# A two-layer block for 32 short sequences on one core: one identity product per step, epsilon added on GpSimd, and a new order of all engines' work

## The reference

```python
# layer 1: a transformer block with modulation by c
shift1, scale1, gate1, shift2, scale2, gate2 = split(silu(c) @ w_ada + b_ada, 6)
k, q, v = split((ln(x) * (1 + scale1) + shift1) @ w_qkv, 3)      # 16 heads of 8 features
y = softmax(q / 8 @ k.T) @ v
x = x + gate1 * (y @ w_proj + b_proj)
x = x + gate2 * (gelu((ln(x) * (1 + scale2) + shift2) @ w_mlp1 + b_mlp1) @ w_mlp2 + b_mlp2)
# layer 2: graph attention, in two directions d, over the first 20 nodes
self = [x, c where the row sum of x is not 0] @ W_self.T + b_self
for d in 0, 1:
    A = adj if d == 0 else adj transposed over its two node axes
    w = softmax(where(A.sum(-1) > 0, q_d k_d / sqrt(8), -9e15) + A @ w_bias + b_bias)
    out_d = per head: (w @ self[:20]) @ Wout[d] + bout[d]
x = x + relu(self + out_0 + out_1)
# ln(x) = (x - mean) * rsqrt(var + 1e-6), over the 128 features
```

## Time and profile before

| | |
|---|---|
| three timed runs | 95.29, 95.89, 96.32 us (median 95.89) |
| the profiled execution, whole | 96.85 us |
| its span on the core | 95.1 us |
| PE busy | 82.7 us |
| DVE busy | 71.7 us |
| POOL busy | 49.0 us |
| ACT busy | 41.8 us |

### The profile page before, as it was taken

The page is one execution under the profiler, slowest core; times in us unless marked ns, Lnnn a source line. Parts: engine busy times, 40 slices in busy tenths (PEclk is TensorE's granted clock), DMA queues, the critical chain, the costliest instruction groups (busy, mean ns, idle before and its releaser), DMA issues.

```text
span 95.1 us, 4068 instructions
## 1 busy us (share of the span) xinstructions
PE 82.7 (87%) x1773; PEld 65.6 (69%) x1773; DVE 71.7 (75%) x181; ACT 41.8 (44%) x96; POOL 49.0 (52%) x60
## 2 busy tenths in 40 slices
...
DMA packets 3890, 5.75 MB, mean 60 GB/s; under 512 B 704, under 2 KB 3008, under 8 KB 3744
## 3 DMA queue, kind: packets, MB, share of 16 engines
...
...
HBM read 4.22 MB, written 0.52 MB: 50 GB/s over the span
## 4 chain that ended last, share of the span: by engine, by line
PE 74%; DVE 7%; issue 7%; ACT 4%; DMA 3%; POOL 1%; POOLq 1%; SPq 0%; ACTq 0%
PE ps_s L1030 12%; PE ps_b L971 7%; PE ps_b L945 7%; PE ps_b L965 7%; PE ps_b L894 5%; PE ps_b L1041 5%; PE ps_b L1066 5%; PE ps_b L1044 4%; PE ps_b L982 4%; PE ps_b L978 4%; DMA w_ada_sb<-in_w_ada 3%; PE ps_b L984 3%; PE ps_b L1074 2%; PE ps_b L921 2%; PE ps_b L953 2%
## 5 line engine op out<-in xcount | busy, mean ns | idle before, releaser
L1173 ACT ACTIVATE PT<-ps_b 120x384 f32<-120x384 f32 x16 | 7.2, 489 | 15.0 <-PE ps_b L1041 15.0
L755 POOL TENSOR_TENSOR Kb<-k_raw,head_mask 128x640 f32<-128x640 f32 x6 | 7.7, 1293 | 9.1 <-DVE k_raw L1273 4.7
L855 POOL TENSOR_TENSOR rstd<-var_eps,minus_half 128x2 f32<-128x2 f32 (+1 forms) x9 | 6.0, 671 | 8.6 <-DVE var_eps L1206 8.5
L723 POOL TENSOR_TENSOR E<-E,neg_max 128x640 f32<-128x640 f32 x7 | 8.9, 1271 | 0.9 <-DVE neg_max L1363 0.8
L1116 ACT ACTIVATE hidden<-ps_b,cols 128x256 f32<-128x256 f32 x16 | 7.1, 476 | 4.7 <-PE ps_b L965 4.7
L945 PE MATMUL ps_b<-xm,w_qkv_sb 128*128 128x256 f32 (+1 forms) x30 | 8.6, 418 | 0.0
L965 PE MATMUL ps_b<-xm,w_rest_sb 128*128 128x256 f32 x32 | 8.4, 381 | 0.0
L1066 PE MATMUL ps_b<-Vz,PT 120*32 120x54 f32 (+1 forms) x384 | 6.6, 216 | 2.1 <-issue 2.1
L1066 PEld LDWEIGHTS ps_b<-Vz,PT 120*32 120x32 f32 (+1 forms) x384 | 5.5, 116 | 4.0 <-issue 3.4
L1101 ACT ACTIVATE Kb<-ps_b,head_mask 128x256 f32<-128x256 f32 (+1 forms) x20 | 7.3, 440 | 1.9 <-PE ps_b L945 1.8
L1030 PE MATMUL ps_s<-Kb,home_b 32*32 32x80 f32 x512 | 8.0, 251 | 0.0
(11 more groups left out here) (109 smaller groups left out, 190.9 us busy)
## 6 DMA issues: line engine op xcount, KB each, us to landing
...
```

The source lines that it names most:

```text
L723: return engine.tensor_tensor(e, e, less_max(key), ALU.add)
L755: return engine.tensor_tensor(Kb1[:, m % K1_RING, d, :, 0:(g1 - g0) * UB, :].rearrange("p i b k -> p i (b k)"), k1_raw[:, d, bs, :].rearra ...
L1173: ins = act.activation(PT[0:KR, r, 0:CH, :], ps[0:KR, 0:CH * P].rearrange("p (j t) -> p j t", t=P), ACT.Exp)
```

## The change

- `rstd` on POOL now has two instructions: the epsilon is added there (then a wait for its own result, then the power), and DVE no longer has its epsilon instruction nor the wait before it.
- A `warm` step is one identity product, not two; there are 14 steps in place of 3, and `WARM` is 13 in place of 11.
- `ON`, `BANKS` and `ORDER` have new contents: every engine's work is ordered anew, and some stages have moved between DVE, ACT and POOL (below, those that the prediction speaks of).

```diff
-WARM = 11
-ON = {'adjf': 'pool',
+WARM = 13
+ON = {'adjf': 'act',
...
- 'resid1': 'pool',
+ 'resid1': 'dve',
...
- ('apply', 0): 'dve',
- ('bhead', 0): 'act',
- ('k1mask', (0, 1)): 'dve',
- ('k1mask', (1, 1)): 'dve',
...
+ ('adjf', 1): 'pool',
+ ('apply', 0): 'pool',
+ ('k1mask', (0, 0)): 'dve',
+ ('k1mask', (1, 0)): 'dve',
...
- ('spread', ('v1', 1, 0)): 'act',
- ('spread', ('v1', 2, 1)): 'act',
- ('spread', ('v1', 3, 1)): 'act',
+ ('shift', (0, 3)): 'dve',
+ ('spread', ('v1', 2, 0)): 'act',
...
- ('sub', 7): 'dve',
...
- ('zero', 'pad'): 'dve',
+ ('zero', 'v0_ones'): 'dve',
...
+ ('take', (('cmod', 0), 0)), ('rstd', (0, 2)), ('warm', 0), ('warm', 1), ('dense', ('xnT', 0)),
...
@@ -852,6 +852,7 @@
                     g0, g1 = norm_chunk(layer, p)
                     for s in fresh("pool", ("stats", key), ("consts", 0)):
                         pool.wait_ge(*s)
+                    wait_own(pool.tensor_scalar(var_eps[:, layer, g0:g1], meanvar[:, layer, g0:g1, 1], LN_EPS, None, ALU.add))
                     ins = pool.tensor_tensor(rstd[:, layer, g0:g1], var_eps[:, layer, g0:g1], minus_half[:, 0:g1 - g0],
                                              ALU.pow)
@@ -997,8 +998,7 @@
                 elif stage == "warm":
-                    for i in range(2):
-                        ins = pe.transpose(ps_s[:, i, 0:P], ident[:, :], ident[:, :])
+                    ins = pe.transpose(ps_s[:, key % HJ, 0:P], ident[:, :], ident[:, :])
@@ -1201,10 +1201,7 @@
                     ins = dve.bn_aggr(meanvar[:, layer, g, :], stats[:, layer, g, :])
-                wait_own(ins)
-                v = meanvar[:, layer, g0:g1, 1]
-                return dve.scalar_tensor_tensor(out=var_eps[:, layer, g0:g1], in0=v, scalar=LN_EPS, in1=v, op0=ALU.add,
-                                                op1=ALU.max)
+                return ins
```

More of the change, by code:

```diff
@@ L230 @@
  ('take', (('yT', 3), 0)): 'act',
[L231 to L234, removed]
- ('zero', 'pad'): 'dve',
+ ('ya', 0): 'dve',
+ ('ya', 4): 'dve',
+ ('ya', 6): 'dve',
+ ('zero', 'v0_ones'): 'dve',
  ('zero', 'v1_ones'): 'dve'}
 BANKS = {('cmod', 0): 0,
[L238 to L242, removed]
+ ('cmod', 1): 1,
+ 'qz': 2,
+ ('bias', 0): 3,
+ ('xnT', 0): 1,
+ ('q', 0): 3,
  ('k', 0): 2,
@@ L265 @@
  ('turn', 2): 1,
[L266 to L279, removed]
+ ('values', 2): 3,
+ ('turn', 3): 3,
+ ('turn', 4): 0,
+ ('values', 3): 0,
+ ('turn', 5): 3,
+ ('turn', 6): 0,
+ ('values', 4): 1,
+ ('turn', 7): 1,
+ ('turn', 8): 1,
+ ('values', 5): 2,
+ ('turn', 9): 2,
+ ('turn', 10): 0,
+ ('values', 6): 1,
+ ('turn', 11): 0,
  ('turn', 12): 0,
- ('values', 7): 0,
+ ('values', 7): 1,
  ('turn', 13): 1,
[L283 to L286, removed]
+ ('turn', 14): 3,
+ ('values', 8): 2,
+ ('turn', 15): 2,
+ ('turn', 16): 2,
  ('values', 9): 3,
@@ L290 @@
  ('values', 10): 1,
[L291 to L294, removed]
+ ('turn', 19): 2,
+ ('turn', 20): 2,
+ ('values', 11): 3,
+ ('turn', 21): 3,
  ('turn', 22): 0,
- ('values', 12): 3,
+ ('values', 12): 1,
  ('turn', 23): 1,
- ('yT', 0): 0,
- ('proj', 0): 0,
- ('x1tok', 0): 0,
+ ('yT', 0): 1,
+ ('proj', 0): 1,
+ ('x1tok', 0): 2,
  ('xn2T', 0): 0,
  ('mlp1', 0, 0): 2,
- ('mlp1', 0, 1): 1,
- ('mlp1', 0, 2): 0,
- ('mlp1', 0, 3): 0,
+ ('mlp1', 0, 1): 0,
+ ('mlp1', 0, 2): 1,
@@ L306 @@
+ ('mlp1', 0, 3): 1,
  ('mlp2', 0): 1,
[L307 to L310, removed]
+ ('rowsum', 0): 0,
+ ('self', 0): 2,
+ ('q1', 0, 0): 2,
+ ('k1', 0, 0): 3,
  ('q1', 0, 1): 1,
- ('k1', 0, 1): 2,
- ('v1', 0): 3,
- ('yT', 1): 1,
- ('proj', 1): 1,
- ('x1tok', 1): 3,
- ('xn2T', 1): 3,
- ('mlp1', 1, 0): 2,
- ('mlp1', 1, 1): 1,
- ('mlp1', 1, 2): 1,
- ('mlp1', 1, 3): 3,
- ('mlp2', 1): 2,
- ('rowsum', 1): 1,
- ('self', 1): 0,
- ('q1', 1, 0): 0,
- ('k1', 1, 0): 2,
- ('q1', 1, 1): 1,
@@ L328 @@
- ('k1', 1, 1): 0,
- ('v1', 1): 0,
- ('yT', 2): 3,
- ('proj', 2): 1,
- ('x1tok', 2): 2,
- ('xn2T', 2): 2,
- ('mlp1', 2, 0): 2,
- ('mlp1', 2, 1): 1,
- ('mlp1', 2, 2): 3,
- ('mlp1', 2, 3): 2,
+ ('k1', 0, 1): 0,
+ ('v1', 0): 1,
+ ('yT', 1): 3,
+ ('proj', 1): 3,
+ ('x1tok', 1): 2,
+ ('xn2T', 1): 2,
+ ('mlp1', 1, 0): 3,
+ ('mlp1', 1, 1): 0,
+ ('mlp1', 1, 2): 2,
+ ('mlp1', 1, 3): 1,
+ ('mlp2', 1): 0,
+ ('rowsum', 1): 0,
+ ('self', 1): 1,
+ ('q1', 1, 0): 1,
+ ('k1', 1, 0): 2,
+ ('q1', 1, 1): 0,
+ ('k1', 1, 1): 3,
@@ L338 @@
+ ('v1', 1): 3,
+ ('yT', 2): 0,
+ ('proj', 2): 3,
+ ('x1tok', 2): 3,
+ ('xn2T', 2): 3,
+ ('mlp1', 2, 0): 3,
+ ('mlp1', 2, 1): 0,
+ ('mlp1', 2, 2): 2,
+ ('mlp1', 2, 3): 1,
  ('mlp2', 2): 2,
  ('rowsum', 2): 3,
[L340 to L341 removed]
+ ('self', 2): 0,
+ ('q1', 2, 0): 0,
  ('k1', 2, 0): 0,
  ('q1', 2, 1): 3,
[L344 to L351 removed]
+ ('k1', 2, 1): 1,
+ ('v1', 2): 3,
```

236 lines of the change are left out of this document (118 added, 118 removed), and 12 rows, old and new, of the table ORDER.

## The result

The change makes the kernel slower. Its median is 99.31 us (98.88 to 102.59, 4 runs) beside 96.10 us for the kernel before: a ratio of 1.033, 95% interval 1.022 to 1.043. A second set of runs gave 1.026 (1.017 to 1.036). My forecast was 94.0 us, in a range of 92.6 to 96.6: wrong in size and in sign.

A forecast was written before the change was run, and what follows sets the result against it. PE was taken as the bound, with late waits for its own instruction blocks and a lowered clock. Terms -0.2 - 0.5 - 0.3 + 0.75 - 1.4 - 0.3 = -1.95 us gave 94.9 for the profiled execution, 94.0 median, range 92.6 to 96.6.

The forecast's parts named there:

- (a): Epsilon on GpSimd: each norm's latency moves by 0.0 to +0.3 us, counted inside (b), (d) and (e).
- (b): Front, 4.5 to 10 us: -0.2 us, with `apply` of chunk 2 later but fewer identity products ahead of k.
- (c): Layer-1 attention, to 26 us: -0.5 us, as the wait for the k evictions goes.
- (d): First norm of layer 2 (mid 1): -0.3 us if `nmr` gets in before `vmask`.
- rival 2: At mid 1, `vmask` on POOL holds `nmr` again, making (d) +1.3 us and the time 95.5; chance 0.27.
- (e): Norm of mid 2: +0.75 us, a PE wait that the change makes.
- (f): Last third: -1.4 us, with waits and clock costing 2.0 us instead of 3.4.
- The part on blocks of instructions: Last third: with a block every 3.7 us at best, only the third of five is short, by 0.8 us.
- the wait behind ACT's DMAs: Last third: ACT issues four DMAs between `exp` of units 8 and 23, so `values` 23 waits about 0.9 us.
- I leave the clock up: Last third: no clock loss counted, since waits are apart and shorter; a fall would cost 1.0 us again.
- (g): Tail: -0.3 us, with the last `ya` on DVE and transpose 3 under the `values`.
- Rival 1: Identity products raise the clock early, PE doing 10 to 13.5 us at 2.4 GHz: -0.7 us, 93.3; chance 0.10.

The follow-up runs named there:

- a_spread_sp: The changed kernel with the first half spread of mid 2 issued by SP and no longer by ACT; 99.40 us, ratio 1.014 to the kernel before.
- fixed: The changed kernel with `stats` 3 behind `nmr` 1, `nmr` of mid 2 behind mid 3's, `vmask` 4 earlier, half spread on SP; 95.72 us, ratio 0.978.
- fixed_few_id: The kernel of fixed with 11 identity products at the start and none later; 95.19 us, ratio 0.978 to the kernel before.
- a_stats: The changed kernel with `stats` of chunk 3 moved behind `nmr` of chunks 2 and 1 on DVE; 98.02 us.

## Why the prediction was wrong, point by point

(a) Epsilon. The instruction takes 0.23 us (I took 0.25). Calling it nothing by itself was wrong: 1.3% either way, depending on the order.

(b) Front, -0.2. The first scores came at 13.54 us, 13.64 before: right in sum, by the wrong sum, and so by luck. `stats` ahead of `nmr` costs 0.5 us and not 0.8 when the load is early (power ready at 6.44 us, `nmr` at 6.97) and over 3 us when it is late, which I left out: I read 4.5 us once as if it were fixed. The early clock gave 0.3 to 0.4 back.

(c) Layer-1 attention, -0.5. The 0.5 us wait went and 1.24 us of the same kind (k evictions) came ahead of the first scores. To the transposes of mid 1 (33.18, before 33.06) the changed kernel is level, although it waits 1.75 us there against 0.92. So about 0.7 us were gained by then, as (b) and (c) say together.

(d) **Mid 1, -0.3: failed, and it was rival 2.** I saw that power and `max` would end together and bet on `nmr`. `vmask` went first by 0.07 us, and it did so in all six profiles of kernels with this order: `nmr` took 2.05 or 2.06 us each time, and PE waited 1.75 us in five and 1.21 in one. That is no coin. What fits is that POOL needs no semaphore to go on and DVE waits for one, the argument that I had written down for the rival and then priced at 0.27. The Trainium skill (SBUF — State Buffer, SBUF: two separate sides) says that the port pair of GpSimd and VectorE is an exclusive lock for the whole instruction, taken by whichever starts first, where the VectorE operation has two inputs in SBUF and the GpSimd one reads SBUF, as here; the 2.05 us agree.

(e) Norm of mid 2, +0.75: too high. It is 0.24 us before mid 2 and 0.40 before mid 3, +0.4 in sum against the 0.22 of before. I had mid 3 done long before; it came directly ahead, and its wait took the other's.

(f) Last third, -1.4: **failed.** The part on blocks of instructions held: I gave 0.8 us for what is left of 2.11, and at that edge it is 0.55 to 1.10 in thirteen of the fourteen profiles of the changed family (in six of them 0.34 to 0.38 more one block on). Two parts failed.

The first is the wait behind ACT's DMAs. It was priced at 0.9 us from 3.28 us for four; they took 4.15 (one of them 1.62), and the wait was 2.03 to 2.09.

The second is "I leave the clock up", an expensive line. In the six profiles that have this wait, the clock falls within 1.5 us behind it in five. In the eight of the changed family without it, it does not fall between 19 and 89 us. But seven of those eight have it low in the tail, from some point between 89.8 and 93.5 us to the end, and in a_spread_sp, fixed and fixed_few_id that begins 1.7 to 2.3 us behind waits of 2.52, 1.90 and 1.54 us. Behind the 1.75 us of mid 1 it fell in two profiles of five, and in none where the wait is gone. In the family of the kernel before it fell within 1.0 us behind a block wait of 1.26 to 1.75 us in three profiles of four. Not each long wait is followed by a fall, so this is a chance and not a rule; but a wait of 2 us must be priced at 2 us plus that chance. I had argued the reverse from the kernel before, where two block waits went before one.

(g) Tail, -0.3: right (from the end of the last `values` to the end of the span 5.0 us against 5.3).

The sum against the earlier trace rows's execution, with what was measured: (b) and (c) together -0.7 up to mid 1 without its wait, (d) +0.8, (e) +0.4, block waits -1.3, spread +2.05, tail -0.3: +0.95. The profile without falls ahead of the tail (a_stats) is at 95.2 us of span, that is +0.1 against 95.1; but the latter has one fall, which I priced at 1.0 us, so +1.1 at equal clock. Two falls bring it to 98.5. Without the 1.0 for the clock my -1.95 is -0.95 in waits, so against this execution I missed by about 2 us in the waits and by about 3 in the clock, with two falls where I had none. In executions with fewer falls the clock's part is smaller.

Rival 1 (0.10) happened in its mechanism, with 0.3 to 0.4 of its 0.7 us at the first scores and no gain in the whole. The Trainium skill (TensorE: Matmul & The Clock Gate, PE-mode transpose), which I had cited against it, says that transpose mode does not count as PE being busy for the clock. This case differs: the products behind 27 identity products ran at 0.26 us, and those behind 11 or 17 at 0.32 to 0.43.

The steps that misled me were a choice between two near-equal starts (d), a price for four DMAs and for what stands behind them (f), and a clock term that was taken as given.
